# First stage of a transformer layer on eight cores: V weights cast by Pool, a fourth x buffer, norms of two tiles interleaved

## The chip, the cores and the metric

The kernel is one program on the 8 cores of one Trainium2 chip. Four sequences are computed, each by two cores: the even core of a pair follows one plan, the odd core another, chosen at the start from an input. No core talks to another. The time is that of the slowest core, in device microseconds. On each core five engines run their own instruction lists in order and meet by semaphores: PE (TensorE, matmuls), DVE (VectorE), ACT (ScalarE), POOL (GpSimd) and SP (here only the issuer of DMAs).

## The reference

```python
x = L0_attn_x                                   # (4, 4096, 2048) f32
# _layernorm(x): (x - mean) / sqrt(var + 1e-5)
x = x + _layernorm(_L0_attn_ref(_layernorm(x), Wq, bq, Wk, bk, Wv, bv, Wo, bo))
x = x + _layernorm(_L0_ffn_ref(_layernorm(x), weight, w_scale, bias))

def _L0_attn_ref(x, ...):                       # 16 heads of 128, causal
    q, k, v = x @ Wq + bq, x @ Wk + bk, x @ Wv + bv
    probs = softmax(q @ k.T * 128 ** -0.5 + causal)
    return concat(probs @ v) @ Wo + bo

def _L0_ffn_ref(x, weight, w_scale, bias):      # per-token int8 quantization
    scale = max(absmax(x), 1e-7) / 127
    q = round(x / scale)
    return (q @ weight.T) * scale * w_scale + bias
```

## The kernel before

Tokens are taken in tiles of 128. The even plan has 21 key tiles (NK) and 21 query tiles (NQ), the odd plan 32 and 11. The kernel runs through these stages.

The first stage is the one that is changed most. For each key tile t, SP loads 128 x 2048 f32 of x into `xin`, a ring of three buffers. DVE takes statistics (`norm_of`: four BN_STATS, BN_AGGR), adds epsilon into `c_ve`; ACT takes the root (`c_sd`); DVE makes the reciprocal (`c_rs`) and the negated mean times it (`c_nm`); ACT writes the normalized tile in bf16 (`xln`, two buffers). PE transposes it in 16 blocks (`transposes`), ACT evicts them into `xT` in two halves, which holds all normalized tokens transposed for the rest of the kernel. Then come V jobs: `v_job(grp, t)` is 16 matmuls of 512 columns that accumulate tile t times the V weights of a group of four heads. DVE evicts a job with its bias into `vst` (`v_out`), and SP stores it to memory (`store_v`). There are four groups and two weight buffers `wv`, so groups 0 and 1 come first: for t under V2_AT only the job of group 0, from V2_AT on those of both groups, and after the last tile the jobs of group 1 that are missing. POOL issues the loads of the weights, f32 in memory and bf16 in `wv`, cast by the DMA. Group 0 is asked for when the first x tile is in, the four quarters of group 1 when tiles 0, 2, 4 and 6 are normalized.

What sets the order is the order in which the code is written, one list per engine. PE: transposes(0); then for each t transposes(t+1), v_job(0, t), and from V2_AT on v_job(1, t). DVE: `x_stats` of tiles 0 to 2; then for each t v_out(0, t), x_stats(t+3), and from V2_AT on v_out(1, t). `x_stats` is the whole norm of a tile on DVE, and it holds DVE while ACT takes the root. ACT: for each t root, normalization, two evictions. The `Seen` helper drops waits that an earlier wait of the same engine has covered.

Then PE computes K and Q of head 0 (`kq_matmul`), the V jobs of groups 2 and 3, and the attention, in whose steps the K and Q of the next head are fitted as filler. The last stage takes query tiles one by one: output projection, norm, residual, norm, quantization, int8-valued matmul, norm, residual, store. Its three norms per tile are made by `norm_of` and `norm_end` with the tag "c" on DVE and by `deviation` on ACT.

Of the kernel before, what the change touches and what calls it, by code (L numbers as in the profile page):

```python
# [7 lines left out]
F32 = mybir.dt.float32  # L8
BF16 = mybir.dt.bfloat16
I8 = mybir.dt.int8  # L10
ALU = mybir.AluOpType
# [17 lines left out]
V2_AT = 10  # L29


class Plan:
# [163 lines left out]
    def frees(self, lo, hi):  # L196
# [29 lines left out]
        + ["x_in%d" % i for i in range(3)]  # L226
        + ["bn_a", "ve_a", "sd_a", "rs_a", "nm_a", "ln_a", "tp_mm", "tp_ev"]
# [6 lines left out]
        + ["o_mm", "bn_o", "bn_c", "bn_l", "ag_a", "ag_c", "mv_c", "ve_c", "sd_c", "rs_c", "nm_c",  # L234
# [18 lines left out]
def build_nc():  # L253
# [26 lines left out]
    with contextlib.ExitStack() as top:  # L280
# [21 lines left out]
        c_ve = at("c_ve", [128, 1], F32, small + 1792)  # L302
# [23 lines left out]
        xin = at("xin", [128, 3, C], F32, A + 32 * KB)  # L326
# [91 lines left out]
        def sync_program(sp, pl):  # L418
# [36 lines left out]
            def load_x(t):  # L455
                if t >= 3:
                    w.wait_ge("ln_a", t - 2)
                sp.dma_start(out=xin[:, t % 3, :], in_=x_seq[t * 128:(t + 1) * 128, :]
                             ).then_inc(S["x_in%d" % (t % 3)], 16)
# [12 lines left out]
            sp.dma_start(out=ident[:, :], in_=masks_in[:, 0:128]).then_inc(S["id_in"], 16)  # L472
            load_x(1)
            load_bv(0)
            load_x(2)
# [3 lines left out]
            for t in range(NK):  # L479
                if t + 4 < NK:  # L480
                    load_x(t + 4)
                if 4 <= t < 4 + NG - 1:
                    load_bv(t - 3)
# [82 lines left out]
        def gpsimd_program(g, pl):  # L566
# [42 lines left out]
            w.wait_ge("x_in0", 16)  # L609
            for k in range(4):  # L610
                load_wv(0, k)
            for k in range(4):
                w.wait_ge("ln_a", 1 + 2 * k)
                load_wv(1, k)
# [55 lines left out]
        def tensor_program(pe, pl):  # L670
# [19 lines left out]
            def v_job(grp, t):  # L690
                b = open_job(pl.job_no[("v", grp, t)])
                w.wait_ge("tp_ev", 2 * t + 2)
                for kc in range(KC):
                    w.wait_ge("wv%d%d" % (grp % 2, kc // 4), 16 * (grp // 2 + 1))
# [194 lines left out]
        def scalar_program(a, pl):  # L889
            w = Seen(a, S)  # L890
            NK, NQ, NC, N = pl.NK, pl.NQ, pl.NC, pl.N
            for t in range(NK):
                w.wait_ge("ve_a", t + 1)
                if t >= 1:
                    w.wait_ge("rs_a", t)
                a.activation(c_sd[:, :], c_ve[:, :], AF.Sqrt).then_inc(S["sd_a"], 1)
                w.wait_ge("nm_a", t + 1)
                if t >= 2:
                    w.wait_ge("tp_mm", 2 * (t - 1))
                w.wait_ge("x_in%d" % (t % 3), 16 * (t // 3 + 1))  # L900
                a.activation(xln[:, t % 2, :], xin[:, t % 3, :], AF.Identity,
                             bias=c_nm[:, t % 4:t % 4 + 1], scale=c_rs[:, t % 4:t % 4 + 1]
                             ).then_inc(S["ln_a"], 1)
                for u in (2 * t, 2 * t + 1):
# [3 lines left out]
                                 ).then_inc(S["tp_ev"], 1)  # L908

# [27 lines left out]
            def deviation(i):  # L937
                w.wait_ge("ve_c", i + 1)
# [55 lines left out]
        def vector_program(v, pl):  # L994
# [46 lines left out]
            def x_stats(t):  # L1041
                w.wait_ge("x_in%d" % (t % 3), 16 * (t // 3 + 1))
                if t >= 1:
                    w.wait_ge("nm_a", t)
# [413 lines left out]
```

## Time and profile before

| | |
|---|---|
| time, median of 3 runs | 2281.61 us (2279.97 to 2284.14) |
| profiled execution: its own time, its span | 2282.92 us, 2281.3 us (core 2) |
| spans of the even cores | 2266.5, 2281.3, 2267.1, 2270.8 us |
| spans of the odd cores | 2208.8, 2200.1, 2210.7, 2207.5 us |
| busy of core 2: PE, DVE, ACT, POOL | 2114.4, 1393.0, 995.4, 247.1 us |
| DMA: hardware queue, software queue | 124.38 MB, 41.95 MB |

The profile is one execution, seen on the slowest core. A busy PE counts matmuls at either clock, so a matmul at half the clock is twice as long and still busy. A row of a timeline has the start, the time, the engine, the line of the kernel and the operation with output and input; "x16" is a merged run of that many instructions, whose time runs from the first start to the last end. What stands in brackets is how long the engine had been idle before it and who released it. V jobs are line 695, transposes line 681, the K and Q matmuls line 708.

### The profile page before, as it was taken

Reading aid. Unit: us, or ns where it says so; the run is one execution under the profiler, and the core shown is the slowest. Engines: PE = TensorE matmul, PEld = TensorE weight load, DVE = VectorE, ACT = ScalarE, POOL = GpSimd, SP = SyncE. Lnnn points to the kernel's source line nnn. Section 1 sums busy time; section 2 is a strip of 40 time slices with the busy share of each in tenths; the row PEclk is TensorE's granted clock in tenths of the full one; section 3 lists DMA queues with packets and bytes.
Section 4 is the critical chain, followed back from the end, with each engine's and each line's share of the span. In section 5 each row is a group of like instructions: output and inputs, shape, how many; then the busy total and the mean of one; then the engine's idle time right before and its main releaser. Section 6 shows DMA issues by size and latency. Waiting matters only on the chain.

```text
span 2281.3 us, 35443 instructions; the slowest of 8 cores (2200.1 to 2281.3 us)
## 1 busy us (share of the span) xinstructions
PE 2114.4 (93%) x11037; PEld 979.2 (43%) x11252; DVE 1393.0 (61%) x2486; ACT 995.4 (44%) x1437; POOL 247.1 (11%) x444
## 2 busy tenths in 40 slices
PE   4799999999999999999999999997889999999995
PEld 2454444444444444444444444443334444444442
DVE  4552321566666676667766666676566666666666
ACT  4550000556555555565556555655423232322322
POOL 0000100011011101110111011103011111111112
PEclk9899999999999999999999999999999999999997
DMA  8643321121121012101210121084143333333332
GB/s 222 192 146 85 60 63 39 31 42 25 24 42 40 15 36 41 40 16 35 42 40 11 40 41 40 13 167 176 59 152 93 97 97 111 111 111 107 91 84 80
DMA packets 167393, 168.68 MB, mean 74 GB/s; under 512 B 135842, under 2 KB 146594, under 8 KB 158498
## 3 DMA queue, kind: packets, MB, share of 16 engines
q1 hardware_dynamic: 157412, 124.38, 18.6%
q0 software_dynamic: 9792, 41.95, 9.1%
q8 instruction: 99, 1.62, 0.3%
q14 instruction: 90, 0.74, 0.1%
HBM read 140.61 MB, written 44.04 MB: 81 GB/s over the span
## 4 chain that ended last, share of the span: by engine, by line
PE 56%; DVE 19%; issue 11%; ACT 9%; DMA 3%; DVEq 1%; POOL 0%; ACTq 0%; SPq 0%; POOLq 0%
PE ps L708 21%; PE ps L695 12%; PE ps L743 8%; PE ps L760 7%; DVE bn L1035 7%; PE ps L774 3%; DVE rb L1139 2%; DVE d_am L1214 2%; ACT wrk L981 2%; ACT wrk L945 2%; ACT fo L952 2%; ACT wrk L971 2%; DVE rb L1137 1%; DMA wv<-wv_p 1%; PE ps L802 1%
## 5 line engine op out<-in xcount | busy, mean ns | idle before, releaser
L933 ACT ACTIVATE P<-ps,negb 128x512 bf16<-128x512 f32 (+2 forms) x1104 | 677.9, 617 | 494.9 <-PE ps L743 483.4
L708 PE MATMUL ps<-xT,wqk 128*128 128x384 bf16 (+1 forms) x2996 | 740.1, 354 | 3.5
L708 PEld LDWEIGHTS ps<-xT,wqk 128*128 128x128 bf16 x3072 | 297.6, 98 | 261.6 <-issue 5.4
L743 PE MATMUL ps<-kq 128*128 128x512 bf16 (+2 forms) x1086 | 377.9, 348 | 11.2 <-ACT P L933 9.4
L760 PE MATMUL ps<-P,v_sb 128*128 128x512 bf16 (+3 forms) x1073 | 368.9, 346 | 15.3 <-DVE P L1117 12.9
L883 PE MATMUL ps<-xT,qx 128*128 128x512 bf16 x1317 | 297.9, 384 | 16.1 <-DMA qx<-qn 14.7
L695 PE MATMUL ps<-wv,xT 128*128 128x512 bf16 x1312 | 302.0, 389 | 9.0 <-DMA wv<-wv_p 7.2
L867 PE MATMUL ps<-xT,yj 128*128 128x512 bf16 x1191 | 286.7, 393 | 1.5 <-issue 0.2
L883 PEld LDWEIGHTS ps<-xT,qx 128*128 128x128 bf16 x1344 | 132.7, 99 | 178.3 <-issue 23.8
L695 PEld LDWEIGHTS ps<-wv,xT 128*128 128x128 bf16 x1344 | 133.1, 100 | 169.1 <-issue 22.1
L1070 DVE TENSOR_SCALAR kq<-ps,bqk 128x384 bf16<-128x384 f32 (+1 forms) x192 | 131.0, 683 | 104.3 <-PE ps L708 103.0
L867 PEld LDWEIGHTS ps<-xT,yj 128*128 128x128 bf16 x1216 | 122.3, 101 | 152.1 <-issue 18.8
L1137 DVE RECIPROCAL rb<-ps 128x192 f32<-128x192 f32 (+1 forms) x96 | 149.2, 1554 | 53.9 <-PE ps L785 53.4
L743 PEld LDWEIGHTS ps<-kq 128*128 128x128 bf16 x1104 | 108.2, 98 | 155.9 <-issue 77.8
L1055 DVE TENSOR_TENSOR vst<-ps,bvb 128x512 bf16<-128x512 f32 x84 | 58.1, 691 | 186.4 <-PE ps L695 186.3
L666 POOL TENSOR_TENSOR fo<-fo,fb 128x512 f32<-128x512 f32 x80 | 102.8, 1297 | 583.8 <-DVE fo L1237 583.8
L941 ACT ACTIVATE c_sd<-c_ve 128x1 f32<-128x1 f32 x63 | 12.8, 203 | 350.3 <-DVE c_ve L1022 350.3
L760 PEld LDWEIGHTS ps<-P,v_sb 128*128 128x128 bf16 x1104 | 108.5, 98 | 129.3 <-issue 38.7
L1117 DVE TENSOR_TENSOR P<-P,tri 128x128 bf16<-128x128 bf16 x336 | 73.1, 225 | 124.3 <-ACT P L933 122.5
L1139 DVE RECIPROCAL rb<-ps 128x192 f32<-128x192 f32 (+1 forms) x96 | 145.2, 1512 | 0.0
L595 POOL TENSOR_TENSOR bt<-qm,km 128x1 f32<-128x1 f32 x96 | 18.5, 192 | 1000.4 <-DVE km L1107 994.0
L774 PE MATMUL ps<-P,ones 128*32 128x512 bf16 (+2 forms) x1104 | 93.8, 352 | 13.7 <-DVE lo L1127 13.7
(91 smaller groups left out, 1632.3 us busy)
## 6 DMA issues: line engine op xcount, KB each, us to landing
xin<-x_seq SPq DMA_DIRECT2D x21, 1024.0 KB, 6.3
x<-x_seq SPq DMA_DIRECT2D x21, 1024.0 KB, 5.7
out<-x SPq DMA_DIRECT2D x20, 1024.0 KB, 3.8
v_g<-vst SPq DMA_DIRECT2D x84, 128.0 KB, 1.7
v_sb<-v_g SPq DMA_DIRECT2D x16, 672.0 KB, 4.7
yj<-yt_h SPq DMA_DIRECT2D x21, 512.0 KB, 6.9
wv<-wv_p POOLq DMA_DIRECT2D x16, 512.0 KB, 10.0
wqk<-wq_p POOLq DMA_DIRECT2D x16, 512.0 KB, 5.2
```

The lines of the kernel that those rows point to most:

```text
L695: mm = pe.matmul(ps[:, b, :], xt_cols(pl, t, 1, kc), wv[grp % 2][:, kc, :], start=(kc == 0), stop=(kc == KC - 1))
L708: mm = pe.matmul(ps[:, JOB + job % 2, 0:n * 128], wqk[p][:, 0 if kind == "q" else 1, kc, :], xt_cols(pl, a, n, kc), start=(kc == 0), stop= ...
L743: pe.matmul(ps[:, S_BANK + s % 2, q0 * 128:n * 128], k_cols(pl, h, kt, 1), q_cols(pl, h, a + q0, n - q0), start=True, stop=True).then_inc( ...
L760: pe.matmul(ps[:, Y_BANK + n % 2, q0 * 128:m], v_sb[h % 2][:, kt, :], P[:, s % RP, q0 * 128:m], start=(v == 0), stop=(v == len(pl.keys[c]) ...
L774: mm = pe.matmul(ps[32 * q:32 * q + 32, DEN, q0 * 128:m], ones[:, 0:32], P[:, (s - v + u) % RP, q0 * 128:m], start=(u < gr), stop=(u >= le ...
L867: mm = pe.matmul(ps[:, n, :], yj[:, j % 2, hc, :], wo_cols(n, hc), start=False, stop=(hc == H - 1))
L883: mm = pe.matmul(ps[:, n if j == NQ - 1 else 4 + n, :], qx(pl, j)[:, kc, :], w8_cols(n, kc), start=(kc == 0), stop=(kc == KC - 1))
L933: a.activation(P[:, s % RP, q0 * 128:m], ps[:, S_BANK + s % 2, q0 * 128:m], AF.Exp, bias=negb[:, k:k + 1], scale=SCALE).then_inc(S["exp_ok ...
L1035: v.bn_stats(bn6[:, k, :], src[:, k * 512:(k + 1) * 512]).then_inc(S["bn_" + tag], 1)
L1070: v.tensor_scalar(dst, ps[:, JOB + job % 2, 0:n * 128], bqk[:, b:b + 1], None, ALU.add).then_inc(S["job_ev"], 1)
L1137: v.reciprocal(rb[:, 0:m // 2], ps[:, MISC, 0:m // 2]).then_inc(S["rec_ok"], 1)
L1139: v.reciprocal(rb[:, m // 2:m], ps[:, MISC, m // 2:m]).then_inc(S["misc_rd"], 1)
```

## The change

Five things are changed. The V weights of groups 0 and 1 are loaded plain, as f32, by SP's queue into four staging areas (`stage`, in a part of `xT` that holds tiles from the 24th on), and POOL casts each quarter into `wv` (semaphore `wc`). SP issues them between the first x tiles, and those of group 1 in iterations 5, 7, 9 and 11 of its loop. The ring of x has four buffers in place of three. The norm of the first stage is split in two: `x_begin` (statistics and aggregation, into one of two buffers `mva`) and `x_end` (reciprocal and negated mean), and DVE does x_end of one tile and then x_begin of the next. The root adds epsilon itself, as its bias, in the first stage and in the last; the DVE instruction that added it goes everywhere. And V2_AT is 14 in place of 10. ACT takes one root ahead of time, on a constant. PE's list is the same but for V2_AT and the semaphore that it waits for.

DVE's list in the first stage, at the first V jobs of the kernel before (line 1055 evicts a V job; 1035, 1018, 1022, 1026, 1028 are a tile's norm):

```order
L1055 TENSOR_TENSOR vst<-ps,bvb 128x512 [waits job_mm,bv0]
L1035 BN_STATS bn_51<-xin 128x6 [waits x_in0,nm_a]
L1035 BN_STATS bn_51<-xin 128x6 x3
L1018 BN_AGGR mv<-bn_51 128x2 [waits bn_a]
L1022 TENSOR_SCALAR c_ve<-mv 128x1 [waits ag_a]
L1026 RECIPROCAL c_rs<-c_sd 128x1 [waits sd_a]
L1028 TENSOR_SCALAR c_nm<-mv,c_rs 128x1 [waits rs_a]
L1055 TENSOR_TENSOR vst<-ps,bvb 128x512 [waits job_mm]
L1035 BN_STATS bn_51<-xin 128x6 [waits x_in1,nm_a,ln_a]
L1035 BN_STATS bn_51<-xin 128x6 x3
L1018 BN_AGGR mv<-bn_51 128x2 [waits bn_a]
```

The same place of the changed kernel (line 1105 evicts a V job; 1094 and 1096 are `x_end`, 1084 and 1087 `x_begin`):

```order
L1105 TENSOR_TENSOR vst<-ps,bvb 128x512 [waits job_mm,bv0]
L1094 RECIPROCAL c_rs<-c_sd 128x1 [waits sd_a]
L1096 TENSOR_SCALAR c_nm<-mva,c_rs 128x1 [waits rs_a]
L1084 BN_STATS bn_51<-xin_77 128x6 [waits x_in3,ag_a,nm_a]
L1084 BN_STATS bn_51<-xin_77 128x6 x3
L1087 BN_AGGR mva<-bn_51 128x2 [waits bn_a]
L1105 TENSOR_TENSOR vst<-ps,bvb 128x512 [waits job_mm]
L1094 RECIPROCAL c_rs<-c_sd 128x1 [waits sd_a]
L1096 TENSOR_SCALAR c_nm<-mva,c_rs 128x1 [waits rs_a]
L1084 BN_STATS bn_51<-xin_74 128x6 [waits x_in0,ag_a,nm_a]
L1084 BN_STATS bn_51<-xin_74 128x6 x3
```

Before, the norm of tile 3 follows the eviction of job 0, whole. Now the end of the norm of tile 2 follows it and after that the statistics of tile 3; the end of the norm of tile 3 stands behind the eviction of job 1.

ACT's list at the same tiles, before (896 the root, 901 the normalization, 906 the evictions):

```order
L896 ACTIVATE c_sd<-c_ve 128x1 [waits ve_a,rs_a]
L901 ACTIVATE xln<-xin,c_nm,c_rs 128x2048 [waits nm_a,x_in2]
L906 ACTIVATE xT<-tp 128x8x128 [waits tp_mm] x2
L896 ACTIVATE c_sd<-c_ve 128x1 [waits ve_a,rs_a]
L901 ACTIVATE xln<-xin,c_nm,c_rs 128x2048 [waits nm_a,x_in0]
L906 ACTIVATE xT<-tp 128x8x128 [waits tp_mm] x2
```

and changed (916 the root, 924 the normalization, 937 the evictions):

```order
L924 ACTIVATE xln<-xin_76,c_nm,c_rs 128x2048 [waits nm_a,x_in2]
L916 ACTIVATE c_sd<-mva,eps 128x1 [waits ag_a,rs_a]
L937 ACTIVATE xT<-tp 128x8x128 [waits tp_mm] x2
L924 ACTIVATE xln<-xin_77,c_nm,c_rs 128x2048 [waits nm_a,x_in3]
L916 ACTIVATE c_sd<-mva,eps 128x1 [waits ag_a,rs_a]
L937 ACTIVATE xT<-tp 128x8x128 [waits tp_mm] x2
L924 ACTIVATE xln<-xin_74,c_nm,c_rs 128x2048 [waits nm_a,x_in0]
```

The root of a tile has moved from right before its normalization to behind the normalization of the tile ahead of it.

SP's list from its start, changed (461 loads x, 468 a quarter of the V weights, 478 the V bias):

```order
L461 DMA xin_74<-x_seq 128x2048
L482 DMA ident<-masks_in 128x128
L468 DMA stage<-wv_p 128x2048 x2
L461 DMA xin_75<-x_seq 128x2048
L468 DMA stage<-wv_p 128x2048 x2
L461 DMA xin_76<-x_seq 128x2048
L478 DMA bvb<-bv_b 128x512
L490 DMA tri<-masks_in 128x128
L491 DMA bqk<-bqk_cols 128x32
L461 DMA xin_77<-x_seq 128x2048
```

Before, no weights were in this list; now two quarters stand ahead of the second x tile and two ahead of the third.

```diff
@@ -26,7 +26,7 @@
 SB = 10
-V2_AT = 10
+V2_AT = 14
...
@@ -323,7 +322,11 @@
         wv = [at("wv%d" % s, [128, KC, 512], BF16, A + 16 * KB * s) for s in range(2)]
-        xin = at("xin", [128, 3, C], F32, A + 32 * KB)
+        xin = [at("xin%d" % i, [128, C], F32, A + o * KB) for i, o in enumerate((32, 40, 48, 76))]
+
+        stage = at("stage", [128, 4, 4 * 512], F32, base + 24 * KC * 128 * 2)
+        mva = at("mva", [128, 2, 2], F32, small + 2880)
+        warm = at("warm", [128, 1], F32, small + 2912)
         xln = at("xln", [128, 2, C], BF16, A + 56 * KB)
@@ -453,10 +456,17 @@
             def load_x(t):
-                if t >= 3:
-                    w.wait_ge("ln_a", t - 2)
-                sp.dma_start(out=xin[:, t % 3, :], in_=x_seq[t * 128:(t + 1) * 128, :]
-                             ).then_inc(S["x_in%d" % (t % 3)], 16)
+                if t >= 4:
+                    w.wait_ge("ln_a", t - 3)
+                sp.dma_start(out=xin[t % 4][:, :], in_=x_seq[t * 128:(t + 1) * 128, :]
+                             ).then_inc(S["x_in%d" % (t % 4)], 16)
+
+            def load_wv(grp, k):
+
+                if grp == 1:
+                    w.wait_ge("wc", k + 1)
+                sp.dma_start(out=stage[:, k, :], in_=wv_p[grp, :, k * 2048:(k + 1) * 2048]
+                             ).then_inc(S["ws%d" % k], 16)
@@ -470,15 +480,21 @@
             sp.dma_start(out=ident[:, :], in_=masks_in[:, 0:128]).then_inc(S["id_in"], 16)
+            load_wv(0, 0)
+            load_wv(0, 1)
             load_x(1)
+            load_wv(0, 2)
+            load_wv(0, 3)
+            load_x(2)
             load_bv(0)
-            load_x(2)
             sp.dma_start(out=tri[:, :], in_=masks_in[:, 128:256]).then_inc(S["const_in"], 16)
                     load_x(t + 4)
+                if t in (5, 7, 9, 11):
+                    load_wv(1, (t - 5) // 2)
                 if 4 <= t < 4 + NG - 1:
@@ -606,12 +622,13 @@
             bound_order = pl.bound_order
-            w.wait_ge("x_in0", 16)
-            for k in range(4):
-                load_wv(0, k)
-            for k in range(4):
-                w.wait_ge("ln_a", 1 + 2 * k)
-                load_wv(1, k)
+            for grp in range(2):
+                for k in range(4):
+                    w.wait_ge("ws%d" % k, 16 * (grp + 1))
+                    g.tensor_copy(wv[grp][:, 4 * k:4 * k + 4, :],
+                                  stage[:, k, :].rearrange("p (k n) -> p k n", n=512)
+                                  ).then_inc(S["wc"], 1)
+            w.wait_ge("ln_a", pl.NK)
             load_wqk(0)
@@ -691,7 +708,10 @@
                 for kc in range(KC):
-                    w.wait_ge("wv%d%d" % (grp % 2, kc // 4), 16 * (grp // 2 + 1))
+                    if grp < 2:
+                        w.wait_ge("wc", 4 * grp + kc // 4 + 1)
+                    else:
+                        w.wait_ge("wv%d%d" % (grp % 2, kc // 4), 16)
                     mm = pe.matmul(ps[:, b, :], xt_cols(pl, t, 1, kc), wv[grp % 2][:, kc, :],
@@ -889,23 +909,40 @@
             NK, NQ, NC, N = pl.NK, pl.NQ, pl.NC, pl.N
-            for t in range(NK):
-                w.wait_ge("ve_a", t + 1)
+            def deviation_a(t):
+                w.wait_ge("ag_a", t + 1)
                 if t >= 1:
                     w.wait_ge("rs_a", t)
-                a.activation(c_sd[:, :], c_ve[:, :], AF.Sqrt).then_inc(S["sd_a"], 1)
+                a.activation(c_sd[:, :], mva[:, t % 2, 1:2], AF.Sqrt, bias=eps[:, :]
+                             ).then_inc(S["sd_a"], 1)
+
+            def normalize(t):
                 w.wait_ge("nm_a", t + 1)
                     w.wait_ge("tp_mm", 2 * (t - 1))
-                w.wait_ge("x_in%d" % (t % 3), 16 * (t // 3 + 1))
-                a.activation(xln[:, t % 2, :], xin[:, t % 3, :], AF.Identity,
+                w.wait_ge("x_in%d" % (t % 4), 16 * (t // 4 + 1))
+                a.activation(xln[:, t % 2, :], xin[t % 4][:, :], AF.Identity,
                              bias=c_nm[:, t % 4:t % 4 + 1], scale=c_rs[:, t % 4:t % 4 + 1]
                              ).then_inc(S["ln_a"], 1)
+
+            w.wait_ge("cst", 1)
+            a.activation(warm[:, :], eps[:, :], AF.Sqrt)
+            deviation_a(0)
+            normalize(0)
+            for t in range(NK):
+                if t == 24:
+                    w.wait_ge("wc", 8)
                 for u in (2 * t, 2 * t + 1):
                                  ).then_inc(S["tp_ev"], 1)
+                if t < 2:
+                    deviation_a(t + 1)
+                if t + 1 < NK:
+                    normalize(t + 1)
+                if 1 <= t < NK - 2:
+                    deviation_a(t + 2)
@@ -935,10 +972,10 @@
             def deviation(i):
-                w.wait_ge("ve_c", i + 1)
+                w.wait_ge("ag_c", i + 1)
                 if i >= 1:
                     w.wait_ge("rs_c", i)
-                a.activation(c_sd[:, :], c_ve[:, :], AF.Sqrt).then_inc(S["sd_c"], 1)
+                a.activation(c_sd[:, :], mv[:, 1:2], AF.Sqrt, bias=eps[:, :]).then_inc(S["sd_c"], 1)
@@ -1000,6 +1037,7 @@
             v.memset(rnd[:, :], ROUND)
+            v.memset(eps[:, :], LN_EPS)
             v.memset(c127[:, :], 127.0).then_inc(S["bo_a"], 1)
@@ -1012,15 +1050,12 @@
-            stats = {"a": 0, "c": 0}
+            stats = {"c": 0}
             def norm_end(parts, i, tag):
-                v.bn_aggr(mv[:, :], parts[:, :, :]).then_inc(S["ag_" + tag], 1)
-                w.wait_ge("ag_" + tag, i + 1)
                 if i >= 1:
                     w.wait_ge("sd_" + tag, i)
-                v.tensor_scalar(c_ve[:, :], mv[:, 1:2], LN_EPS, None, ALU.add
-                                ).then_inc(S["ve_" + tag], 1)
+                v.bn_aggr(mv[:, :], parts[:, :, :]).then_inc(S["ag_" + tag], 1)
                 w.wait_ge("sd_" + tag, i + 1)
@@ -1038,13 +1073,28 @@
-            def x_stats(t):
-                w.wait_ge("x_in%d" % (t % 3), 16 * (t // 3 + 1))
+            def x_begin(t):
+                w.wait_ge("x_in%d" % (t % 4), 16 * (t // 4 + 1))
                 if t >= 1:
-                    w.wait_ge("nm_a", t)
+                    w.wait_ge("ag_a", t)
+                if t >= 2:
+                    w.wait_ge("nm_a", t - 1)
+                    w.wait_ge("sd_a", t - 1)
+                for k in range(4):
+                    v.bn_stats(bn6[:, k, :], xin[t % 4][:, k * 512:(k + 1) * 512]
+                               ).then_inc(S["bn_a"], 1)
+                w.wait_ge("bn_a", 4 * t + 4)
+                v.bn_aggr(mva[:, t % 2, :], bn6[:, :, :]).then_inc(S["ag_a"], 1)
+
+            def x_end(t):
+                b = t % 4
+                w.wait_ge("sd_a", t + 1)
                 if t >= 4:
                     w.wait_ge("ln_a", t - 3)
-                norm_of(xin[:, t % 3, :], t, "a")
+                v.reciprocal(c_rs[:, b:b + 1], c_sd[:, :]).then_inc(S["rs_a"], 1)
+                w.wait_ge("rs_a", t + 1)
+                v.tensor_scalar(c_nm[:, b:b + 1], mva[:, t % 2, 0:1], c_rs[:, b:b + 1], -1.0,
+                                ALU.mult, ALU.mult).then_inc(S["nm_a"], 1)
@@ -1161,12 +1211,16 @@
-            for t in range(3):
-                x_stats(t)
+            for t in range(2):
+                x_begin(t)
+                x_end(t)
+            x_begin(2)
             for t in range(NK):
                 v_out(0, t)
+                if t + 2 < NK:
+                    x_end(t + 2)
                 if t + 3 < NK:
-                    x_stats(t + 3)
+                    x_begin(t + 3)
                 if t >= V2_AT:
```

## Rows read from the trace of the kernel before

**Rows 1.** Spans by core: us from first to last instruction, granted clock.
```profile
core 2: 2281.3 us, clock 0.974
...
core 5: 2210.7 us, clock 0.984
```

**Rows 2.** Timeline, 0 to 40 us: start, us, engine, line, operation, [idle before, releaser].
```profile
7.63 2.47 DVE L1035 BATCH_NORM_STATS2 bn<-xin 128x6 f32<-128x512 f32 x4 [2.58 <-DMA xin<-x_seq]
...
10.81 1.28 ACT L896 ACT_TABLE_LOAD   x1 [10.81 <-DVE c_ve L1022]
...
13.04 2.09 ACT L901 ACTIVATE xln<-xin,c_nm,c_rs 128x2048 bf16<-128x2048 f32 x1 [0.73 <-DVE c_nm L1028]
...
34.88 1.86 PE L695 MATMUL ps<-wv,xT 128*128 128x512 bf16 x4 [5.84 <-DMA wv<-wv_p]
```

**Rows 3.** Windows: PE, PEld, DVE, ACT, POOL busy (count), PE clock, DMA share, GB/s.
```profile
4.50:34.80 30.30, 8.17 (x44) 4.67 (x44) 10.23 (x27) 11.82 (x11) 3.38 (x6) 0.93 1.03 261
...
120.00:140.00 20.00, 19.89 (x116) 9.99 (x116) 11.43 (x26) 11.42 (x12) 0.00 (x0) 1.00 0.46 146
```

**Rows 4.** Timeline of one tile of the first stage, from an eviction to the transposes.
```profile
94.04 0.69 DVE L1055 TENSOR_TENSOR vst<-ps,bvb 128x512 bf16<-128x512 f32 x1 [3.58 <-PE ps L695]
94.41 1.94 ACT L906 ACTIVATE xT<-tp 128x1024 bf16<-128x1024 bf16 x2 [1.70 <-PE tp L681]
...
94.65 2.46 DVE L1035 BATCH_NORM_STATS2 bn<-xin 128x6 f32<-128x512 f32 x4
...
98.19 0.17 DVE L1026 RECIPROCAL c_rs<-c_sd 128x1 f32<-128x1 f32 x1 [0.45 <-ACT c_sd L896]
98.46 0.22 DVE L1028 TENSOR_SCALAR c_nm<-mv,c_rs 128x1 f32<-128x1 f32 x1
...
98.83 2.09 ACT L901 ACTIVATE xln<-xin,c_nm,c_rs 128x2048 bf16<-128x2048 f32 x1 [0.74 <-DVE c_nm L1028]
...
101.06 1.05 PE L681 MATMUL tp<-ident,xln 128*128 128x128 bf16 x16 [2.85 <-ACT xln L901]
```

**Rows 5.** Timeline of PE, 60 to 125 us: transposes and job behind a wait.
```profile
70.62 1.05 PE L681 MATMUL tp<-ident,xln 128*128 128x128 bf16 x16 [2.85 <-ACT xln L901]
71.51 5.30 PE L695 MATMUL ps<-wv,xT 128*128 128x512 bf16 x16
...
86.74 1.87 PE L681 MATMUL tp<-ident,xln 128*128 128x128 bf16 x16 [5.58 <-ACT xln L901]
88.40 5.46 PE L695 MATMUL ps<-wv,xT 128*128 128x512 bf16 x16
```

**Rows 6.** Timeline of PE: two jobs per tile at full clock; the start of K/Q.
```profile
118.35 1.06 PE L681 MATMUL tp<-ident,xln 128*128 128x128 bf16 x16
...
126.15 1.06 PE L681 MATMUL tp<-ident,xln 128*128 128x128 bf16 x16
...
222.24 4.06 PE L708 MATMUL ps<-xT,wqk 128*128 128x384 bf16 x22
```

**Rows 7.** Timeline of one query tile in the last stage.
```profile
1979.95 2.06 ACT L971 ACTIVATE wrk<-ps,c_nm,c_rs 128x2048 f32<-128x2048 f32 x1 [0.74 <-DVE c_nm L1028]
...
1982.16 0.38 PE L864 MATMUL ps<-bohl,sel 128*128 128x512 bf16 x1 [1.98 <-ACT wrk L971]
...
2008.97 0.26 DVE L1018 BATCH_NORM_AGGREGATE mv<-bn 128x2 f32<-128x24 f32 x1
2009.34 0.15 DVE L1022 TENSOR_SCALAR c_ve<-mv 128x1 f32<-128x1 f32 x1
2009.65 0.20 ACT L941 ACTIVATE c_sd<-c_ve 128x1 f32<-128x1 f32 x1 [5.57 <-DVE c_ve L1022]
...
2010.59 2.06 ACT L971 ACTIVATE wrk<-ps,c_nm,c_rs 128x2048 f32<-128x2048 f32 x1 [0.74 <-DVE c_nm L1028]
```

**Rows 8.** Groups by line (busy us, mean ns, idle before): the root of the last stage.
```profile
L941 ACT ACTIVATE c_sd<-c_ve 128x1 f32<-128x1 f32 x63 | 12.8, 203 | 350.3 <-DVE c_ve L1022 350.3
```

**Rows 9.** Timeline of POOL: a cast of 2048 columns, and a two-input form.
```profile
1562.39 2.16 POOL L656 CAST bohl<-bof 1x2048 bf16<-1x2048 f32 x1
1564.70 4.05 POOL L658 TENSOR_TENSOR bohl<-bof,bhi 1x2048 bf16<-1x2048 f32 x1
```

More of the change, by code:

```diff
@@ L225 @@
         + ["wv%d%d" % (s, k) for s in range(2) for k in range(4)] + ["bv%d" % g for g in range(NG)]
-        + ["x_in%d" % i for i in range(3)]
-        + ["bn_a", "ve_a", "sd_a", "rs_a", "nm_a", "ln_a", "tp_mm", "tp_ev"]
+        + ["x_in%d" % i for i in range(4)] + ["ws%d" % i for i in range(4)] + ["wc"]
+        + ["bn_a", "sd_a", "rs_a", "nm_a", "ln_a", "tp_mm", "tp_ev"]
         + ["job_mm", "job_ev"] + ["vs%d" % i for i in range(4)] + ["vl0", "vl1"]
@@ L233 @@
         + ["cw_in", "cf_in", "bo_in", "bo_a", "bo_ok", "yj0", "yj1", "xc0", "xc1", "xc2", "xc3"]
-        + ["o_mm", "bn_o", "bn_c", "bn_l", "ag_a", "ag_c", "mv_c", "ve_c", "sd_c", "rs_c", "nm_c",
+        + ["o_mm", "bn_o", "bn_c", "bn_l", "ag_a", "ag_c", "sd_c", "rs_c", "nm_c",
            "ln2", "x1_ok", "ln3", "am_ok", "sc_ok", "rc_ok", "qt_ok", "qn_ok", "qx0", "qx1",
@@ L301, in build_nc @@
         mv = at("mv", [128, 2], F32, small + 1760)
-        c_ve = at("c_ve", [128, 1], F32, small + 1792)
         c_sd = at("c_sd", [128, 1], F32, small + 1824)
```

## The prediction

> **What bounds the kernel now.** Four views were read, in this order. The spans by core come first [rows 1]: core 2 sets the time, and the slowest odd core ends 70 us before it. So only the even plan counts (21 key tiles, 21 query tiles), whatever the odd cores gain or lose up to that distance. The profiled execution took 2282.9 us round a span of 2281.3, against a median of 2281.6 for the runs; the sums below are made on the profiled one, and 1.3 us are taken off at the end.
>
> The second view is the first stage in order of time. PE waits in two ways there. At the start it waits for V weights: the last quarter of group 0 lands at 34.9 us, while the DMA engines are fully busy from 4.5 us on [rows 2, 3]. After that it waits for normalized tiles: a transpose starts when ACT has written xln, and the wait before it is 2.85 us in the tile shown [rows 4]. What it loses in all is found by subtraction. At full clock one iteration with two V jobs and one transpose step takes 7.80 us [rows 6], the transposes take 0.89 of it (70.62 to 71.51 [rows 5]), so a V job is 3.455 us. From the end of the first job (34.88 + 1.86 = 36.74) to the first K/Q matmul (222.24) are 185.5 us; 41 jobs (141.7) and 19 transpose steps (16.9) are work; 26.9 us are waits and slow clock. Where there are two jobs per tile nothing is lost (the clock is 1.00 there [rows 3]), and behind the stage PE is the busy engine for a long time, so what the stage ends later or earlier goes into the time whole.
>
> The third view is the last stage, one query tile in 30.64 us [rows 7]. PE waits 1.98 us of each for ACT, and the chain that sets the period runs through DVE and ACT alone, through three norms per tile.
>
> **The change, part by part.**
>
> *Earlier weights.* Before the first job can end, x tiles 0 and 1 and the four quarters must land. x 0 is there at 7.6; five more loads of 1.05 MB stand in SP's queue up to the last quarter. The stretch 4.5 to 34.8 moved 261 GB/s as written, 7.9 MB, and some 2.6 MB of it were cast on the way from twice as many bytes read: 10.5 MB read in 30.3 us, 3.0 us for a load of 1.05 MB [rows 3]. The last quarter lands at 7.6 + 15 = 22.6. Pool's cast of 2048 columns took 2.16 us on one partition, and 4.05 us in a form with two inputs [rows 9]; I take 2.1, with 4.05 as the other end, and 0 as the lower bound. All four pipeline behind the loads, so one cast counts: 24.7. x 1 lands at 16.6, its norm ends about 6.2 us later (13.04 + 2.09 - 7.63 less the 1.28 us table load, which the added root on eps takes away beforehand [rows 2]), and the transposes end at 24.5. The job follows at a mostly slow clock, 5.3 us [rows 5]: end at 30.0, against 36.7. **Gain 6.8 us**, between 11 and 2.
>
> *The order of the norms.* In the order shown with the change, DVE evicts job (0, t) and only then does the reciprocal and the negated mean of tile t+2; before, it did those of tile t+3 there. DVE works in order, ACT's normalization of t+2 waits for them, and PE's transposes of t+2 stand ahead of job (0, t+1). So while there is one job per tile nothing is left for PE between the end of job (0, t) and the transposes of t+2. Queued behind the waiting DVE instruction are only the statistics of t+3, needed a period later, and behind PE's transposes stands all of PE. The gap in pieces [rows 4]: eviction starts 0.1 after the job, the next DVE instruction 0.61 later (94.04 to 94.65), reciprocal to mean 0.27, mean to normalization 0.37, normalization to transposes 2.23 (98.83 to 101.06). Sum **3.6 us**. The old order had 2.85 every second tile, since one norm lay one job further ahead; taking the statistics out of the chain (94.65 to 98.19, 3.5 us) saves less than the job (3.455) and transposes that the chain lost as cover. With V2_AT = 14 there are 14 such single jobs (t = 0 to 13), each with a gap behind it: 14 x 3.6 = 50.4. For t = 14 to 18 the second job covers 3.455 of 3.6: 5 x 0.15 = 0.7.
>
> *The clock.* PE's rows show that a gap has an echo. After 2.85 us of waiting, transposes and job took 6.0 us (1.05 and 5.30, overlapping), where 4.35 is the work; after 5.58 us they took 6.95 [rows 5]. Those are matmuls at 1.2 instead of 2.4 GHz for part of the job. 3.6 lies between: 1.65 + (0.75 / 2.73) x 0.95 = 1.9; as the full-speed job that stood between two gaps goes, I take **2.0 us** per gap, 14 x 2.0 = 28; the ends are 0 and 2.6 (36).
> The Trainium skill ("TensorE: Matmul & The Clock Gate", Part 1) says that an idle TensorE falls back to half rate, with which the rows agree, and that for modelling the ramp's penalty is under 1% of a typical kernel's span. By that rule the term would be under 22.8 us rather than 28 and the time at most about 2306; the kernel before with its few gaps stays inside it, 14 longer ones by the rows don't.
>
> *Four x buffers.* x(t+4) is now asked for about two periods before its statistics; no wait for x is left, and x is off PE's chain. Its old share is in the 26.9 us. The second group's quarters are loaded in iterations 5 to 11 at some 10 us each and cast long before iteration 14: nothing. The warm-up root, eps' memset and the semaphores: nothing, they lie before x 0 has landed at 7.6 [rows 2]; uncovered they would cost the 1.28 us of the table load at most.
>
> *Epsilon as bias, in the last stage.* Each norm loses one DVE instruction. Now aggregation starts at 2008.97, the add at 2009.34, the root at 2009.65: 0.68 us [rows 7]. Without the add ACT's root should start 0.16 after the aggregation's 0.26: an ACT start lies 0.16 behind the end of the DVE instruction it waits for, as 2009.34 + 0.15 to 2009.65. That is 0.42, **0.26 us less** per norm; bounds 0 and 0.37. 63 norms [rows 8], of which I count 61 on the chain: -15.9 us, ends 0 and -23. PE's 1.98 us of slack per tile [rows 7] is more than the 0.78 that goes, so PE doesn't take over.
>
> *The sum.* Stage: 50.4 + 0.7 + 28 = 79.1 of loss in place of 26.9, less 6.8 at the start: +45.4. Last stage: -15.9. Net +29.5 on 2282.9 is 2312.4, and on the runs' median 2311. The stage would end near 268 in place of 222.
>
> **The rivals.**
> *The clock stays up.* If gaps had no echo, the term of 28 goes: +1.5, 2283 us, no change. Against it: both waits shown, the shorter and the longer, are followed by a slow stretch. 5%.
> *The norms do run ahead.* The mechanism: the reciprocal and mean of a tile ready before the job ahead of its transposes ends. Then PE waits for ACT alone, whose evictions (1.94), normalization (2.09), root (0.20) [rows 4, 7] and starts come to 4.95 us a tile against 4.35 of PE work: 14 x 0.6 = 8.4 of loss in place of 26.9. With 6.8 and 15.9: -41, 2240 us, faster. It decides as soon as nm of t+2 comes before the eviction of job (0, t) on DVE. For it speaks that statistics and end are split apart, and that ACT has its root early; against it the row order on DVE, which puts the eviction first. It is the case on the other side. 7%.
> *The start costs more and the echo is longest.* Casts at 4.05 us and loads slowed by each other eat the 6.8, and slow stretches last 2.6: +6.8 + 8.4, 2326. The cast on 128 partitions isn't in the trace of before. 14%.
> *The last stage gives nothing,* because the root with a bias tile waits as long as the add did: +45.4, 2327 us. Against it: ACT's other activations read bias and scale tiles and start 0.16 after DVE just the same. 6%.
>
> **How the numbers follow.** Forecast 68%: 2311, its own range 2301 to 2321 (the echo 1.5 to 2.4 per gap, -7 and +6; the last stage 12 to 20). The range for 8 in 10 takes in the slower rivals and half of the way to the clock rival: 2290 to 2328; what is left out is the two cases at or below 2283 and a little at the top. A measurement of this kernel tells 0.2% (4.6 us) from no change. Faster is the second rival and a part of the first in which the last stage gives 23: 8%. Same is the rest of the first and a little of the forecast's low tail: 5%. Slower: 87%.
>
> **What would show it.** In the changed kernel's timeline of 40 to 140 us: a PE wait of 3.5 to 3.7 us before every transpose step, released by ACT's normalization, about 10 us from one to the next, and the granted clock below 0.9 all along, where it was 1.00 by 120 us [rows 3]. The normalization in turn is released by DVE's mean, and this by PE's job. The first K/Q matmul near 268. The first eviction near 30. Pool casts near 2 us. In the last stage the period falls from 30.6 to 29.9 and the root starts about 0.42 after the aggregation. Wrong would be a PE wait of under 1 us in the single-job stretch (second rival), a slow stretch missing behind gaps (first), or an unchanged period in the last stage (fourth).

## The result: 2317.8 us, 1.6% slower

| | before | changed |
|---|---|---|
| median of the runs | 2281.2 us | 2317.8 us (2316.5 to 2321.0, 4 runs) |
| ratio, 95% interval | 1 | 1.0161 (1.0143 to 1.0178) |
| span of core 2, profiled | 2281.3 us | 2316.5 us |
| first K/Q matmul, cores 0, 2, 4, 6 | 213, 222, 213, 214 us | 260, 261, 259, 261 us |
| first to last exponential (attention) | 1203, 1209, 1204, 1206 us | 1207, 1215, 1208, 1207 us |
| first to last root of the last stage | 649, 648, 648, 649 us | 641, 639, 641, 639 us |

The forecast was 2311 with a range of 2290 to 2328. Later runs shared their chips with runs of the kernel before whose medians were 2279 to 2281 us; their ratios are the ones to compare. Some executions of every kernel were over 1.5% longer, at a lower granted clock on one die or on both, and are left out of all times and ratios below.

The spans by core of the changed kernel, against [rows 1]: the even cores are still the late ones.

```profile
core 2: 2316.5 us, clock 0.977
...
core 5: 2246.8 us, clock 0.985
```

The start, from the timeline of the changed kernel, against [rows 2]:

```profile
5.18 1.28 ACT L929 ACT_TABLE_LOAD   x1 [5.18 <-DVE sel L1050]
...
11.74 2.09 ACT L924 ACTIVATE xln<-xin,c_nm,c_rs 128x2048 bf16<-128x2048 f32 x1 [0.74 <-DVE c_nm L1096]
...
15.32 2.47 DVE L1084 BATCH_NORM_STATS2 bn<-xin 128x6 f32<-128x512 f32 x4 [3.74 <-DMA xin<-x_seq]
...
22.45 1.90 POOL L628 CAST wv<-stage 128x2048 bf16<-128x2048 f32 x1 [2.03 <-DMA stage<-wv_p]
...
23.24 5.07 PE L715 MATMUL ps<-wv,xT 128*128 128x512 bf16 x16
```

x tile 1 is there at 15.3 and the last quarter at 22.4, the cast takes 1.90 us on 128 partitions, and the first V job ends at 28.3 in place of 36.7. What follows is a period of the single-job stretch, against [rows 4]:

```profile
76.02 0.69 DVE L1105 TENSOR_TENSOR vst<-ps,bvb 128x512 bf16<-128x512 f32 x1 [5.89 <-PE ps L715]
76.62 0.15 DVE L1094 RECIPROCAL c_rs<-c_sd 128x1 f32<-128x1 f32 x1
...
76.88 0.21 DVE L1096 TENSOR_SCALAR c_nm<-mva,c_rs 128x1 f32<-128x1 f32 x1
...
77.25 2.09 ACT L924 ACTIVATE xln<-xin,c_nm,c_rs 128x2048 bf16<-128x2048 f32 x1 [4.85 <-DVE c_nm L1096]
```

Read it as a chain without a break: DVE waited 5.89 us for the job, the reciprocal starts 0.60 after the eviction, the mean 0.26 later, the normalization 0.37 later. ACT had been idle for 4.85 us until then, although x had long landed. PE's own timeline shows the end of it, and the clock, against [rows 5, 6]:

```profile
79.49 1.05 PE L698 MATMUL tp<-ident,xln 128*128 128x128 bf16 x16 [3.65 <-ACT xln L924]
80.38 5.30 PE L715 MATMUL ps<-wv,xT 128*128 128x512 bf16 x16
89.33 1.05 PE L698 MATMUL tp<-ident,xln 128*128 128x128 bf16 x16 [3.65 <-ACT xln L924]
90.22 3.62 PE L715 MATMUL ps<-wv,xT 128*128 128x512 bf16 x16
97.48 1.56 PE L698 MATMUL tp<-ident,xln 128*128 128x128 bf16 x16 [3.65 <-ACT xln L924]
98.83 4.82 PE L715 MATMUL ps<-wv,xT 128*128 128x512 bf16 x16
...
164.61 1.05 PE L698 MATMUL tp<-ident,xln 128*128 128x128 bf16 x16 [0.19 <-ACT xln L924]
...
260.91 9.67 PE L728 MATMUL ps<-xT,wqk 128*128 128x384 bf16 x48
```

All 14 gaps behind single jobs are there (3.58 to 3.65 us, the first 3.90). Behind the five tiles that follow, each with two jobs, they are 0.2, and 0.8 once. Of the 13 single jobs that stand behind a gap three take 3.6 us and ten take 4.7 to 5.3. No x tile is waited for after the first four. The first K/Q matmul comes at 260.9, where the forecast had 268. In the last stage, first the reciprocal of the kernel before, behind the root shown there, then the changed kernel:

```profile
2009.95 0.17 DVE L1026 RECIPROCAL c_rs<-c_sd 128x1 f32<-128x1 f32 x1 [0.45 <-ACT c_sd L941]
```

```profile
1897.69 0.29 ACT L978 ACTIVATE c_sd<-mv,eps 128x1 f32<-128x1 f32 x1 [5.31 <-DVE mv L1058]
...
1927.82 0.29 ACT L978 ACTIVATE c_sd<-mv,eps 128x1 f32<-128x1 f32 x1 [5.31 <-DVE mv L1058]
...
2018.10 0.26 DVE L1058 BATCH_NORM_AGGREGATE mv<-bn 128x2 f32<-128x24 f32 x1
2018.51 0.29 ACT L978 ACTIVATE c_sd<-mv,eps 128x1 f32<-128x1 f32 x1 [5.31 <-DVE mv L1058]
2018.91 0.17 DVE L1061 RECIPROCAL c_rs<-c_sd 128x1 f32<-128x1 f32 x1 [0.54 <-ACT c_sd L978]
...
2021.75 0.38 PE L884 MATMUL ps<-bohl,sel 128*128 128x512 bf16 x1 [1.77 <-ACT wrk L1008]
```

The root starts 0.41 after the aggregation, as forecast. But it takes 0.29 us, where it took 0.20. The two roots at the top are one query tile apart: most tiles have this period of 30.13 us, where it was 30.64 before and the forecast had 29.9.

### The profile page after: what moved, and what is told of

It is laid out like the page before. It is cut to its first block, busy times and chain, and to the rows that moved or that the text cites. A ratio compares the mean times of both kernels' runs of the same rounds, so it can differ in the third digit from the quotient of the medians.

```text
span 2316.5 us, 35527 instructions; the slowest of 8 cores (2245.4 to 2316.5 us)
## 1 busy us (share of the span) xinstructions
PE 2126.6 (92%) x11252; PEld 978.4 (42%) x11252; DVE 1380.4 (60%) x2403; ACT 1004.0 (43%) x1438; POOL 255.9 (11%) x444
## 4 chain that ended last, share of the span: by engine, by line
PE 58%; DVE 17%; issue 10%; ACT 10%; DMA 2%; DVEq 1%; SPq 0%; ACTq 0%; POOL 0%; POOLq 0%
PE ps L728 21%; PE ps L715 12%; PE ps L763 8%; PE ps L780 7%; DVE bn L1070 6%; PE ps L794 3%; DVE rb L1189 2%; DVE d_am L1268 2%; ACT wrk L1018 2%; ACT wrk L982 2%; ACT xln L924 2%; ACT fo L989 2%; ACT wrk L1008 2%; DVE rb L1187 1%; PE ps L822 1%
## 5 line engine op out<-in xcount | busy, mean ns | idle before, releaser
L728 PE MATMUL ps<-xT,wqk 128*128 128x512 bf16 (+1 forms) x3072 | 753.9, 355 | 0.1
L763 PE MATMUL ps<-kq 128*128 128x512 bf16 (+2 forms) x1104 | 386.6, 350 | 9.2 <-ACT P L970 9.2
L780 PE MATMUL ps<-P,v_sb 128*128 128x512 bf16 (+2 forms) x1104 | 382.1, 348 | 13.5 <-DVE P L1167 12.9
L715 PE MATMUL ps<-wv,xT 128*128 128x512 bf16 x1344 | 312.0, 395 | 0.0
L887 PE MATMUL ps<-xT,yj 128*128 128x512 bf16 x1216 | 276.3, 380 | 0.0
L978 ACT ACTIVATE c_sd<-mv,eps 128x1 f32<-128x1 f32 x63 | 18.6, 294 | 336.4 <-DVE mv L1058 336.4
```

The lines of the kernel that those rows point to most:

```text
L715: mm = pe.matmul(ps[:, b, :], xt_cols(pl, t, 1, kc), wv[grp % 2][:, kc, :], start=(kc == 0), stop=(kc == KC - 1))
L728: mm = pe.matmul(ps[:, JOB + job % 2, 0:n * 128], wqk[p][:, 0 if kind == "q" else 1, kc, :], xt_cols(pl, a, n, kc), start=(kc == 0), stop= ...
L763: pe.matmul(ps[:, S_BANK + s % 2, q0 * 128:n * 128], k_cols(pl, h, kt, 1), q_cols(pl, h, a + q0, n - q0), start=True, stop=True).then_inc( ...
L780: pe.matmul(ps[:, Y_BANK + n % 2, q0 * 128:m], v_sb[h % 2][:, kt, :], P[:, s % RP, q0 * 128:m], start=(v == 0), stop=(v == len(pl.keys[c]) ...
L887: mm = pe.matmul(ps[:, n, :], yj[:, j % 2, hc, :], wo_cols(n, hc), start=False, stop=(hc == H - 1))
```

## The experiments

The main theory was that one position in DVE's list makes the loss: the end of a norm behind the eviction of the job that stands ahead of that tile's transposes. The rival was that loads or casts set the pace. Ten runs were made, two of them of the same kernel. The gap, the clock, the weights, the bias and the number of single jobs were each taken alone.

### The end of the norm ahead of the eviction

```diff
             for t in range(NK):
-                v_out(0, t)
                 if t + 2 < NK:
                     x_end(t + 2)
+                v_out(0, t)
```

> The changed kernel, with one pair of DVE steps swapped: the end of the norm of tile t+2 (reciprocal and mean) stands ahead of the eviction of job (0, t) instead of behind it. Theory A (the order on DVE makes the 3.6 us gap): the normalization of t+2 runs while job (0, t) runs, PE waits about 0.6 us per single job because ACT needs about 4.95 us a tile against 4.35 of PE work, the slow clock behind the gaps goes; the first stage ends near 197 us in place of 261, the time falls by about 64 us to 2254, which is also below the kernel before (2281). Rival B (the pace of the first stage is set by loads or by Pool's casts, and the gap only shows up at the transposes): the gap moves but the stage still ends at 255 to 261, the time stays at 2312 to 2318.

Measured: 2281.7 us, ratio 1.0017 (1.0006 to 1.0028): by the ratios 33 us less than the changed kernel and still 4 more than the kernel before. The first K/Q matmul came at 216 to 229 us. Both expectations missed. The loads weren't the pace, since the stage did get shorter, but the gap went only at every second tile. PE's timeline of core 2:

```profile
68.31 1.86 PE L698 MATMUL tp<-ident,xln 128*128 128x128 bf16 x16 [3.66 <-ACT xln L924]
69.97 4.30 PE L715 MATMUL ps<-wv,xT 128*128 128x512 bf16 x16
74.11 1.06 PE L698 MATMUL tp<-ident,xln 128*128 128x128 bf16 x16
```

and all engines over the piece ahead of it:

```profile
61.09 2.46 DVE L1084 BATCH_NORM_STATS2 bn<-xin 128x6 f32<-128x512 f32 x4
...
64.07 0.29 ACT L916 ACTIVATE c_sd<-mva,eps 128x1 f32<-128x1 f32 x1 [5.01 <-DVE mva L1087]
64.27 1.92 ACT L937 ACTIVATE xT<-tp 128x1024 bf16<-128x1024 bf16 x2
...
66.08 2.09 ACT L924 ACTIVATE xln<-xin,c_nm,c_rs 128x2048 bf16<-128x2048 f32 x1
```

ACT sat 5.01 us in front of a root, with evictions ready behind it in its list. That root waits for statistics that DVE starts only after the job's eviction. It is the same fault on a second engine: in ACT's list of the changed kernel, the root of t+2 stands ahead of the evictions of t+1.

### The norms one tile further ahead

```diff
             x_begin(2)
+            x_end(2)
+            x_begin(3)
             for t in range(NK):
                 v_out(0, t)
-                if t + 2 < NK:
-                    x_end(t + 2)
-                if t + 3 < NK:
-                    x_begin(t + 3)
+                if t + 3 < NK:
+                    x_end(t + 3)
+                if t + 4 < NK:
+                    x_begin(t + 4)
...
+            load_x(4)
             for t in range(NK):
-                if t + 4 < NK:
-                    load_x(t + 4)
+                if t + 5 < NK:
+                    load_x(t + 5)
```

> The changed kernel with the norms of the first stage one tile further ahead on DVE: behind the eviction of job (0, t) stand the end of the norm of t+3 and the statistics of t+4 (before: t+2 and t+3), and SP asks for x(t+5) in iteration t. ACT's list is as it was. The run with the end of the norm ahead of the eviction kept a 3.7 us gap at every second tile, because ACT took the root of t+2, which waits for statistics that DVE starts only behind job (0, t-1), ahead of the evictions of t+1. Theory A (the gap is a matter of how many jobs lie between a norm and its use; one more on DVE and ACT's root no longer waits): PE's wait per single job is ACT's 4.95 less PE's 4.35 us, the clock stays up, the stage ends at 195 to 200 in place of 261 us, time about 2253. Rival B (the loads set the pace once the gaps are gone: 1.05 MB of x per 4.95 us are 212 GB/s, and group 1 comes on top): waits for x on DVE, stage ends at 210 to 220, about 2270. Rival C (ACT's order alone is the fault, the position on DVE is not): the 3.7 us gap at every second tile stays, as before 2283.

Two runs, 2254.2 and 2257.6 us. The same code was run again for an interval:

> The kernel with the norms one tile further ahead once more (same code as the run e5_ahead), with more rounds, for a ratio with its interval: it had 2254 and 2258 us. Theory A (the order of the norms was the fault; weights, bias and order then add up): weights -8 to -9, bias -8.5, order -10, against the kernel before (2281) about 2254, ratio 0.988. Rival B (the two times were lucky): 2262 or more.

Measured: 2253.0 us, **ratio 0.9889 (0.9874 to 0.9905)**: 1.1% faster than the kernel before. It differs from the changed kernel in two things: DVE does the end and the statistics of a norm one tile earlier, and one x load is asked for earlier. Theory A. PE's timeline of the first of the two runs (core 2):

```profile
44.50 1.05 PE L699 MATMUL tp<-ident,xln 128*128 128x128 bf16 x16 [0.26 <-ACT xln L925]
45.39 3.62 PE L716 MATMUL ps<-wv,xT 128*128 128x512 bf16 x16
49.27 1.05 PE L699 MATMUL tp<-ident,xln 128*128 128x128 bf16 x16 [0.26 <-ACT xln L925]
```

The gap is 0.26 us and the period 4.77, where 4.95 was expected. First K/Q matmul at 197 to 203 us in both runs. The rival is there in a small way: on core 0 DVE waits 3.0 us for an x tile, with the DMA engines busy all the time from 60 to 90 us, and PE 1.95 us for it in turn (on core 2 PE has one such wait of 2.78):

```profile
82.30 2.47 DVE L1085 BATCH_NORM_STATS2 bn<-xin 128x6 f32<-128x512 f32 x4 [2.99 <-DMA xin<-x_seq]
```

```profile
60.00:90.00 30.00, 26.59 (x188) 14.04 (x189) 22.27 (x48) 24.55 (x24) 5.47 (x3) 1.00 1.00 331
```

(The second fence is a window, with columns as in [rows 3].)

### ACT's normalization ahead of the evictions as well

```diff
             for t in range(NK):
+                if t < 2:
+                    deviation_a(t + 1)
+                if t + 1 < NK:
+                    normalize(t + 1)
...
                 for u in (2 * t, 2 * t + 1):
...
-                if t < 2:
-                    deviation_a(t + 1)
-                if t + 1 < NK:
-                    normalize(t + 1)
```

> The same as the run with norms one tile further ahead, and on ACT the normalization of t+1 stands ahead of the evictions of t, so that ACT doesn't wait for the transposes between the two. Theory A (ACT's chain normalization, transposes, evictions is what is left of the gap): the period of a single-job tile falls from 4.95 to 4.45 us (2.09 + 1.94 + 0.29 and starts), 14 x 0.5 = 7 us less, about 2246. Rival B (loads set the pace by then): no difference to the run before it.

Measured: ratio 0.9897 (0.9865 to 0.9929), no gain over the run without it. That is the number of rival B, but not for its reason: the period was 4.90 us, longer than the 4.77 of the run without it. Now PE waits 0.40 us for the evictions before each job, since these start behind the normalization.

```profile
61.20 0.16 DVE L1095 RECIPROCAL c_rs<-c_sd 128x1 f32<-128x1 f32 x1 [0.63 <-ACT c_sd L917]
...
61.83 2.09 ACT L925 ACTIVATE xln<-xin,c_nm,c_rs 128x2048 bf16<-128x2048 f32 x1 [0.81 <-DVE c_nm L1097]
...
65.89 3.61 PE L716 MATMUL ps<-wv,xT 128*128 128x512 bf16 x16 [0.40 <-ACT xT L942]
```

ACT itself is idle for 0.81 us, waiting for the mean, which waits for the root that ACT took last. The expectation had added up ACT's busy times and left out this round trip.

### Filling the gap

```diff
                 v_job(0, t)
+                if t < V2_AT:
+                    for i in range(13):
+                        pe.matmul(ps[:, DEN, :], xt_cols(pl, t, 1, i), wv[0][:, i, :],
+                                  start=True, stop=True)
```

> The changed kernel, with 13 matmuls of 512 columns put behind each of the 14 single V jobs, into a PSUM bank that nobody reads (2.8 us at full clock, less than the 3.6 us gap). Theory A (the slow stretches behind the gaps are an echo of PE's idling): the granted clock stays 1.00, the period of a single-job tile falls from 9.4 on average to 8.0 us, time 14 x 1.4 = -20, about 2298. Rival B (matmuls are slow there for another reason, such as what DVE, ACT or the DMAs do at that moment): the period stays at 9.4 or grows by the filler's slow matmuls (13 x 0.43 = 5.6 us, 2 us over the gap), 2317 to 2345.

Measured: 2298.6 us, ratio 1.0092 (1.0074 to 1.0109), by the ratios 16 us below the changed kernel, with 182 matmuls more. The first K/Q matmul came at 242, 18 us earlier than there. Windows of 60 to 140 us, core 2: the changed kernel first, then the filled one.

```profile
60.00:140.00 80.00, 50.84 (x283) 25.01 (x281) 29.95 (x65) 35.90 (x35) 7.58 (x4) 0.85 0.55 190
```

```profile
60.00:140.00 80.00, 71.17 (x436) 35.90 (x443) 37.12 (x80) 41.97 (x40) 7.57 (x4) 1.00 0.60 207
```

The granted clock goes from 0.85 to 1.00, the same work needs less time, and the period is 8.15 us, as between two transposes of this run:

```profile
72.17 1.05 PE L698 MATMUL tp<-ident,xln 128*128 128x128 bf16 x16 [0.84 <-ACT xln L928]
...
80.33 1.05 PE L698 MATMUL tp<-ident,xln 128*128 128x128 bf16 x16 [0.84 <-ACT xln L928]
```

 So the slow stretches come from PE's idling: 18 us, or 1.3 us per gap.

### Fewer single jobs

```diff
-V2_AT = 14
+V2_AT = 10
...
-                if t in (5, 7, 9, 11):
-                    load_wv(1, (t - 5) // 2)
+                if t in (1, 3, 5, 7):
+                    load_wv(1, (t - 1) // 2)
```

> The changed kernel with V2_AT 10 in place of 14, as in the kernel before, and group 1's quarters asked for in iterations 1, 3, 5, 7. Theory A (each single job carries one gap of 3.6 us and 1.4 us of slow clock on average, a tile with two jobs carries 0.15): 4 x 4.85 = 19 us less, about 2298, stage ends near 241. Rival B (the stage's length doesn't depend on how many tiles are single, since what is late is a norm per tile): 2317.

Measured: 2297.6 us, ratio 1.0073 (1.0044 to 1.0103); first K/Q matmul at 240 to 242, 19 us earlier on the mean of the even cores, and ten gaps of over 3 us in place of 14. That is 4.8 us for each of the four, against 4.85 expected: the loss is per single job. The ratio's interval is wide, the position of the K/Q matmul isn't.

### The weights alone, and a fourth buffer with them

The kernel before, with the quarters staged by SP and cast by POOL as in the change, but asked for in iterations 1, 3, 5 and 7, and V2_AT left at 10:

> The kernel before, with only the V weights of groups 0 and 1 loaded plain by SP and cast by Pool (group 1 asked for in iterations 1, 3, 5, 7, V2_AT stays 10, three x buffers, the old norm order). Theory A (the start of the change is a gain by itself): the first eviction is at 28 to 30 us in place of 37, nothing else changes, the 15 us wait for an x tile near 65 us is shorter or gone, since the group's quarters are no longer cast by the DMA: -8 to -16, about 2269. Rival B (weights ahead of x in the one SP queue hold the x tiles up, and the gain at the first job is given back by later tiles): 2279 to 2283.

Measured: 2269.4 us, ratio 0.9955 (0.9941 to 0.9970), theory A. The first eviction came at 29.3 us and the first K/Q matmul at 205 to 211 in place of 213 to 222. From the fifth tile on none waited for x. The expectation speaks of a wait of 15 us; in the trace that is the time from the issue to the landing of one x load (14.95 us), and DVE waited 2.28 us of it. The same with `xin` as four buffers (and, as in the change, with the loads of the K and Q weights held until all tiles are normalized; PE doesn't wait for them at the first K/Q matmul):

> The run with only the V weights changed, and the fourth x buffer on top of it, the norms in their old order. Theory A (with the weights out of the way no tile waits for x behind the start, so a fourth buffer brings nothing): the same as with the weights alone, ratio 0.9955 to the kernel before, about 2270. Rival B (the fourth buffer is what takes the x waits away): 3 to 8 us less, about 2265.

Measured: 2271.2 us, ratio 0.9973 (0.9962 to 0.9984), K/Q at 204 to 211. No gain, theory A.

### Epsilon as bias alone

```diff
-                a.activation(c_sd[:, :], c_ve[:, :], AF.Sqrt)
+                a.activation(c_sd[:, :], mv[:, 1:2], AF.Sqrt, bias=eps[:, :])
```

with the add of `norm_end` left out for the tag "c", in the kernel before:

> The kernel before, with epsilon as the bias of the root in the last stage only (the add on DVE left out there, 63 norms). Theory A (root with a bias tile takes 0.29 us instead of 0.20, so a norm gains 0.17 us): last-stage period 30.64 to 30.14 us, time -9 to -10.5, about 2271. Rival B (0.26 us per norm as in the prediction): -16, 2265. Rival C (the changed kernel's shorter last stage has another source, such as another phase of the attention's end): 0, 2281.

Measured: ratio 0.9977 (0.9966 to 0.9989), 5 us (3 to 8); the last stage itself went from a mean of 648.4 to 639.5 us, 8.9 less on the even cores. Theory A by the stage. The whole gained less than the 9 to 10.5 us expected, and no run shows where the rest went.

> The changed kernel with the root of the last stage without its bias, so epsilon is left out of the norms there. Theory A (reading a bias tile is what makes the root take 0.294 us instead of 0.203): the root takes 0.20, the last stage gets shorter by 61 x 0.09 = 5.5 us against the changed kernel. Rival B (the longer time comes from the strided input mv): it stays at 0.29.

One run, 2310.3 us, whose last stage leaves epsilon out. The row of the root, by line, first the changed kernel and then this one:

```profile
L978 ACT ACTIVATE c_sd<-mv,eps 128x1 f32<-128x1 f32 x63 | 18.6, 294 | 336.4 <-DVE mv L1058 336.4
```

```profile
L978 ACT ACTIVATE c_sd<-mv 128x1 f32<-128x1 f32 x63 | 12.8, 203 | 335.7 <-DVE mv L1058 335.7
```

Last stage 633 to 635 us, 6 below the changed kernel: 63 x 0.091 = 5.7. The bias tile makes the difference, not the input, which is the same in both.

## Why the prediction was right, point by point

*The order of the norms* was the main term and is shown: 14 gaps of 3.6 us were forecast and 14 of 3.58 to 3.90 came on core 2, with the releasers named. One more tile of distance takes them away, and four fewer single jobs take away four of them. The gaps sum to 51.1 on core 2 (forecast 50.4), those behind two jobs to 1.6 (0.7). What the prediction missed is that ACT's root stands in the way too. As long as DVE's position makes the gap this doesn't show; with the DVE pair swapped it is the bound.

*The clock*: 2.0 us per gap were taken, 28 in all. From the end of the first job (28.3) to the first K/Q matmul (260.9) are 232.6 us; less 158.6 of work, 51.1 of gaps behind single jobs and 1.6 of the others, 21.3 are left, 1.5 per gap. The filler gives 18 by another way. This is the term of the first stage that was mis-sized, by 6.7. The size was off since one gap in four has no echo: 8.15 us from 89.33 to 97.48, and 9.84 before. The first rival (no echo) is excluded by the filler run. The rule of the Trainium skill ("TensorE: Matmul & The Clock Gate", Part 1), a penalty of under 1% of the span, holds for this term: 21.3 of 2316 is 0.92%. The time that went with it, at most 2306, was passed all the same, since the last stage gave less and the attention took longer.

*The start*: 6.8 us gained by forecast, 8.4 measured (36.7 to 28.3). x tile 1 landed at 15.3 in place of 16.6, and the job took 5.07 in place of 5.3. The size of the cast didn't count: no wait of PE for it is in the rows.

*The last stage* is the other mis-sized term: 15.9 forecast, 8.6 on core 2 and 8.4 on the mean of the even cores. The step was "0.26 us less per norm": the root starts as early as forecast, but a root that reads a bias tile takes 0.294 instead of 0.203, so 0.17 is left, from aggregation to reciprocal 0.98 before and 0.81 now. 61 x 0.17 would be 10.4. On core 2 the first tile gave 0.6 back (37.54 in place of 36.89), and two of the roots start 0.3 late; the rest was not settled. The fourth rival named the bias tile as the risk, and gave it an all-or-nothing price; it cost a third of the gain per norm.

*Not in the prediction*: 5.5 us more in the attention on core 2. Its length is 1203 to 1215 us over all even cores of all profiled executions, the kernel before included, in no order with the edits. The mean of the four even cores is 1205.7 before and 1209.3 changed. Whether any of these 3.6 us belongs to the change was not settled.

The sum on core 2: +38.7 (forecast +45.4), +5.5 (0), -8.6 (-15.9) and 0.4 less in the pieces between and behind these make the +35.2 of the spans. Two errors of about 7 us of opposite sign cancelled. That 2311 came so close is in part luck; the direction and the mechanism are not.

There is one more thing behind the first. Core 2 of the profiled execution before was 8 to 9 us later into K/Q than the other three, so the first stage lost 38.7 us on it, but 46 to 47 on the others (44.6 on the mean of the four). No single wait made it late: near 80 us DVE of core 0 waited 3.73 us for an x tile, that of core 2 only 2.28. The same kernel ran in two patterns. On core 2 a gap of 2.4 to 2.9 us (once 5.6) stood at every second tile, with a slow job behind it [rows 5], 13.4 us for two tiles. On core 0 a gap of 1.2 to 1.5 us stood at every tile, the jobs behind it took 3.62 us, and two tiles took 11.6 to 11.7:

```profile
53.71 1.05 PE L681 MATMUL tp<-ident,xln 128*128 128x128 bf16 x16 [1.43 <-ACT xln L901]
54.60 3.62 PE L695 MATMUL ps<-wv,xT 128*128 128x512 bf16 x16
59.41 1.05 PE L681 MATMUL tp<-ident,xln 128*128 128x128 bf16 x16 [1.20 <-ACT xln L901]
60.30 3.62 PE L695 MATMUL ps<-wv,xT 128*128 128x512 bf16 x16
65.41 1.05 PE L681 MATMUL tp<-ident,xln 128*128 128x128 bf16 x16 [1.49 <-ACT xln L901]
```

From 40 to 110 us the granted clock was 0.95 on core 0 and 0.85 on core 2. Core 6 ran mixed, and had one gap of 2.78 us with a job of 3.62 behind it. What puts a core into one pattern or the other was not tested. The prediction took its loss of 26.9 us and its echo from core 2 alone.

*The second rival* (norms that do run ahead, 2240 us) was rightly ruled out for this order by DVE's list. With the order mended it comes true, at 2253: the last stage gave 8.4 and not 15.9, and two gaps of 4.1 and 0.8 us are left at the start, while the first tiles land.

## What to carry to other kernels

When a step is split so that its halves can be interleaved, count for each consumer how many of its own jobs lie between the producer's last input and the use. A half that is moved behind a wait takes over that wait, whatever it costs itself: here some 0.5 us of DVE work. One place earlier, ahead of the eviction, took 33 us off (ratio 1.0161 to 1.0017), and a whole tile earlier, with the statistics and one load, 62 (0.9889). Read the lists of all engines in the loop for it, since mending one shows the next. And price a gap of PE with its echo: 3.6 us of waiting cost 5.2 on the mean, while the gaps of 1.2 to 1.5 us of the kernel before had none. Read the echo on more than one core.

## What the runs showed of the hardware

A 128 x 1 root on ACT takes 0.203 us without and 0.294 us with a bias tile (63 of each). No run took the bias tile away from an activation of 2048 columns, so what it costs there is not shown.

A POOL cast of 128 x 2048 f32 to bf16 takes 1.90 us, as on one partition (1.88 to 2.16).

An echo of the clock can fall out: behind the same gap of 3.65 us the transposes and the job together took 6.2 us three times and 4.5 the fourth (59.82 to 93.84 us on core 2), in a steady pattern on all even cores.
